# Upper channels stored with one DMA each, and the last six outputs shared among three engines and two queues

## The reference, cut to what matters

```python
x = x + conv(_ln_c(x), w_sym)
t = _to_tokens(x)
# _quantize_activations_groupwise, for a group ag of 3 images:
gamma = jnp.max(jnp.abs(ag))
xq = jnp.clip(ag * 128.0 / (gamma + EPS), -128.0 + EPS, 128.0 - EPS)
# _L0_ffn_ref
h = gelu(quantize(_ln_t(t) @ sign(W1).T + b1))
t = t + quantize(h @ sign(W2).T + b2)
```

## Time and profile before

| | |
|---|---|
| median of 3 runs | 613.7 us (611.32 to 615.29) |
| the profiled execution, its own time | 617.74 us |
| its span, first to last instruction | 615.9 us |
| mean granted clock of TensorE | 0.918 |
| TensorE busy | 496.8 us (81%) |
| VectorE busy | 467.1 us (76%) |
| ScalarE busy | 382.0 us (62%) |
| GpSimd busy | 219.7 us (36%) |
| moved by DMA | 81.29 MB, 132 GB/s over the span |

### The profile page before, as it was taken

How to read it: one execution, slowest core, us unless ns; L and a number is a source line. 1 busy time by engine, 2 the same in 40 slices (tenths; PEclk the granted TensorE clock), 3 DMA queues, 4 the chain that set the end, 5 groups by cost and what they waited for, 6 DMA issues and landing times.

```text
span 615.9 us, 9847 instructions
## 1 busy us (share of the span) xinstructions
PE 496.8 (81%) x3552; PEld 353.5 (57%) x3552; DVE 467.1 (76%) x1041; ACT 382.0 (62%) x598; POOL 219.7 (36%) x221
## 2 busy tenths in 40 slices
PE   2355527999969996758789989998999999987893
PEld 2255527999969995324335545555555555545562
DVE  7987861222228987996799898799989989699675
ACT  2688950000000353637799989998999898989550
POOL 4000000000400002212076747576666567558450
PEclk9666759999979997979999989999999999999798
DMA  8998325566965646940011000122222423263345
GB/s 223 290 316 248 104 61 150 149 175 169 204 161 150 178 124 250 386 157 1 27 51 53 27 27 0 52 82 74 78 74 77 133 78 101 80 230 104 125 135 178
DMA packets 55280, 81.29 MB, mean 132 GB/s; under 512 B 7361, under 2 KB 39105, under 8 KB 55232
## 3 DMA queue, kind: packets, MB, share of 16 engines
q1 hardware_dynamic: 39616, 68.28, 36.5%
q10 hardware_dynamic: 15136, 11.22, 6.5%
q0 software_dynamic: 480, 1.17, 0.9%
HBM read 53.12 MB, written 27.53 MB: 131 GB/s over the span
## 4 chain that ended last, share of the span: by engine, by line
PE 42%; DVE 22%; ACT 18%; DMA 10%; issue 5%; SPq 3%; ACTq 0%; DVEq 0%
PE bank L976 19%; DMA arena<-x 6%; PE bank L1058 5%; ACT arena L566 5%; DVE am L844 5%; ACT arena L560 4%; DMA arena<-kz_d 3%; PE bank L1026 3%; PE bank L1027 3%; PE bank L1028 3%; PE bank L1068 2%; DVE arena L816 2%; DVE arena L831 2%; ACT arena L482 2%; DVE arena L766 2%
## 5 line engine op out<-in xcount | busy, mean ns | idle before, releaser
L435 POOL TENSOR_TENSOR arena<-arena 128x512 f16<-128x512 f32 x159 | 186.9, 1212 | 120.6 <-DVE arena L831 99.3
L976 PE MATMUL bank<-arena 128*128 128x112 f32 (+1 forms) x1152 | 136.1, 283 | 20.8 <-ACT arena L482 12.6
L560 ACT ACTIVATE arena<-bank,b1s 128x512 f32<-128x512 f32 x180 | 125.1, 703 | 42.2 <-PE bank L1028 41.8
L976 PEld LDWEIGHTS bank<-arena 128*128 128x128 f32 x1152 | 135.0, 199 | 21.7 <-ACT arena L482 12.8
L1058 PE MATMUL bank<-arena 128*128 128x512 f16 x360 | 106.4, 390 | 5.4 <-ACT arena L584 3.6
L566 ACT ACTIVATE arena<-arena,gm 128x1024 f32<-128x1024 f32 x90 | 102.7, 1163 | 1.7 <-DVE gm L866 1.7
L844 DVE TENSOR_REDUCE am<-arena 128x1 f32<-128x3072 f32 x30 | 100.3, 3343 | 3.5 <-ACT arena L560 3.5
L750 DVE TENSOR_TENSOR arena<-bank,arena 128x512 f32<-128x512 f32 x48 | 33.2, 691 | 81.0 <-PE bank L976 80.9
L1026 PE MATMUL bank<-arena 128*128 128x512 f16 x180 | 71.0, 395 | 26.0 <-DVE arena L824 17.7
L497 ACT ACTIVATE arena<-arena,wmean 51x576 f16<-51x576 f32 (+1 forms) x10 | 8.6, 856 | 129.0 <-DVE wmean L724 116.2
L1027 PE MATMUL bank<-arena 128*128 128x512 f16 x180 | 70.6, 392 | 0.0
(11 more groups left out here) (118 smaller groups left out, 684.9 us busy)
## 6 DMA issues: line engine op xcount, KB each, us to landing
arena<-park_d SPq DMA_DIRECT2D x44, 384.0 KB, 3.6
arena<-kz_d SPq DMA_DIRECT2D x100, 112.0 KB, 2.9
arena<-kz_d ACTq DMA_DIRECT2D x92, 112.0 KB, 3.4
park_d<-arena SPq DMA_DIRECT2D x6, 1536.0 KB, 14.5
arena<-x SPq DMA_DIRECT2D x8, 1024.0 KB, 8.9
out<-arena SPq DMA_DIRECT2D x32, 256.0 KB, 2.0
kz_d<-arena SPq DMA_DIRECT2D x8, 672.0 KB, 11.0
arena<-x SPq DMA_DIRECT2D x16, 256.0 KB, 9.8
```

The source lines that it names most:

```text
L435: last = pool.tensor_tensor(out=low_half(u, m, m + 1), in0=yslot(u)[:, 2 * m:2 * m + 2, :], in1=hib(u, m, m + 1), op=ALU.subtract)
L560: act.activation(yslot(s)[:, 2 * m:2 * m + 2, :], m1p[c % 2][:, :].rearrange("p (h n) -> p h n", h=2), ACT.Identity, bias=b1s[:, m:m + 1], ...
L976: last = t.matmul(ps[:, :, lo:hi], WB[BUFS[g]][:, 1 - db, c, :], xn[:, :, lo + db:hi + db], start=(db == 0), stop=(db == -1))
```

## The change

Four things are changed. `store_upper` issues one DMA for both quarters, with the destination written as quarter, channel, pixel and the source as 128 partitions; it is used for all 30 units and for image 15, and the counts of the slots' semaphores change from 48 to 32. The two halves of image 15 have a semaphore each. Of the last six units, SyncE issues both stores of 24, 25 and 28, and ScalarE both of 27, 26 and 29. Units 25 and 26 are no longer finished by VectorE: ScalarE copies their turned inputs from PSUM to SBUF (keep_x, at steps 37 and 38, ahead of result(28) and result(29)), multiplies their outputs by the factor once it is known, and GpSimd adds the two. The turned inputs of units 28 and 29 use the banks of 25 and 26, and TensorE waits for the copies (xt) and no longer for fin.

```diff
-        turned = {... ((bank[0], bank[1]), (tA, tB), (m2a, m2b), (xA, xB), (bank[0], bank[1])))}
+        turned = {... ((bank[0], bank[1]), (tA, tB), (m2a, m2b), (bank[0], bank[1]), (tA, tB)))}
+        by_pool = early[0:2]
+        by_act = [early[2], early[1], early[4]]
+        XT = [view(XB + i * OW, OW) for i in range(2)]
+        def made(u):
+            return (fin_g, by_pool.index(u) + 1) if u in by_pool else (fin, u + 1 - sum(k < u for k in by_pool))
         def store_upper(q, u, slot, done):
-            for e in range(2):
-                at = u % 2 * HALF + e * QTR
-                q.dma_start(out[u // 2, P:C, at:at + QTR], Y2[e * C1:(e + 1) * C1, slot, HALF:OW]).then_inc(done, 16)
+            q.dma_start(out[u // 2, P:C, u % 2 * HALF:(u % 2 + 1) * HALF].rearrange("c (e n) -> e c n", e=2),
+                        Y2[:, slot, HALF:OW]).then_inc(done, 16)
 # sync: store(), and the loop
-                if u not in early:
-                    store_upper(sp, u, slot, done)
+                store_upper(sp, u, slot, done)
-                if 0 <= u < FT:
-                    sp.wait_ge(fin, u + 1)
+                if 0 <= u < FT and u not in by_act:
+                    sp.wait_ge(*made(u))
 # gpsimd, at its end
+            for i, u in enumerate(by_pool):
+                pool.wait_ge(xt, 2 * (i + 1))
+                pool.wait_ge(scaled, i + 1)
+                y = Y2[:, u % Y2R, :]
+                pool.tensor_tensor(out=y, in0=y, in1=XT[i], op=ALU.add).then_inc(fin_g, 1)
 # scalar
+            def keep_x(i):
+                act.wait_ge(mm1, MT * FT)
+                act.wait_ge(xpl, i + 1)
+                ta, tb = turn(by_pool[i])
+                act.activation(XT[i][:, 0:HALF], ta[:, :], ACT.Copy).then_inc(xt, 1)
+                act.activation(XT[i][:, HALF:OW], tb[:, 0:QTR], ACT.Copy).then_inc(xt, 1)
+                if FT - 2 <= w < FT:
+                    keep_x(w - FT + 2)
                 if s > FT and 0 <= w < FT:
                     result(w, 0)
-            for u in early:
-                act.wait_ge(fin, u + 1)
+            act.wait_ge(gsc2, FT // GT)
+            for u in by_pool:
+                y = Y2[:, u % Y2R, :]
+                act.activation(y, y, ACT.Copy, scale=gm[:, 9:10]).then_inc(scaled, 1)
+            for u in by_act:
+                b, half = u // 2, u % 2
+                act.wait_ge(*made(u))
+                act.dma_start(out[b, 0:P, half * HALF:(half + 1) * HALF], Y2[:, u % Y2R, 0:HALF]).then_inc(st_o[u % Y2R], 16)
                 store_upper(act, u, u % Y2R, st_o[u % Y2R])
 # vector
             def final(u):
+                if u in by_pool:
+                    return
 # tensor
             for i in (3, 4):
-                pe.wait_ge(fin, early[i] - 3)
+                pe.wait_ge(xt, 2 * (i - 2))
```

More of the change, by code:

```diff
@@ L215, in build @@
         gmx2 = sem("gmx2"); gtr = [sem(f"gtr{i}") for i in range(2)]; gone = [sem(f"gone{i}") for i in range(2)]; gall2 = sem("gall2"); gsc2_t = sem("gsc2_t"); gsc2 = sem("gsc2")
-        xps = sem("xps"); xpl = sem("xpl"); ld_g = [sem(f"ld_g{i}") for i in range(GT - 1)]; fin = sem("fin"); f15 = sem("f15")
-        st_o = [sem(f"st_o{i}") for i in range(Y2R)]; st_f15 = sem("st_f15")
+        xps = sem("xps"); xpl = sem("xpl"); ld_g = [sem(f"ld_g{i}") for i in range(GT - 1)]; fin = sem("fin"); fin_g = sem("fin_g"); xt = sem("xt"); scaled = sem("scaled"); f15 = sem("f15")
+        st_o = [sem(f"st_o{i}") for i in range(Y2R)]; st_f15 = [sem(f"st_f15{h}") for h in range(2)]
         block = ctx.enter_context(nc.Block())
@@ L250, in build @@
         XE = [*XL, *(view(at + i * RB * C, RB * C).rearrange("p (n c) -> p n c", n=RB) for i in range(2))]
-        turned = {v: pair for v, pair in zip(early, ((bank[0], bank[1]), (tA, tB), (m2a, m2b), (xA, xB), (bank[0], bank[1])))}
+        turned = {v: pair for v, pair in zip(early, ((bank[0], bank[1]), (tA, tB), (m2a, m2b), (bank[0], bank[1]), (tA, tB)))}
+        by_pool = early[0:2]
[3 more added lines that the diff above has]
+            return (fin_g, by_pool.index(u) + 1) if u in by_pool else (fin, u + 1 - sum(k < u for k in by_pool))
         def turn(u):
@@ L348, in store @@
                 sp.dma_start(out[b, 0:P, half * HALF:(half + 1) * HALF], Y2[:, slot, 0:HALF]).then_inc(done, 16)
-                if u not in early:
-                    store_upper(sp, u, slot, done)
+                store_upper(sp, u, slot, done)
             for h in range(2):
                 sp.wait_ge(f15, 2 * (h + 1))
-                store(FT + h, Y2R - 2 + h, st_f15)
+                store(FT + h, Y2R - 2 + h, st_f15[h])
             sp.wait_ge(st_pk[KEPT // 2], 16)
@@ L379, in _ @@
             for r in range(Y2R):
-                sp.wait_ge(st_o[r], 48 * len(range(r, FT, Y2R)))
-            sp.wait_ge(st_f15, 96)
+                sp.wait_ge(st_o[r], 32 * len(range(r, FT, Y2R)))
+            for done in st_f15:
+                sp.wait_ge(done, 32)
         @block.gpsimd
@@ L579, in result @@
                     if u >= Y2R:
-                        act.wait_ge(st_o[u % Y2R], 48 * (u // Y2R))
+                        act.wait_ge(st_o[u % Y2R], 32 * (u // Y2R))
                     elif u >= Y2R - 2:
-                        act.wait_ge(st_f15, 48 * (u - Y2R + 3))
+                        act.wait_ge(st_f15[u - Y2R + 2], 32)
                     act.wait_ge(mm2[0], u + 1)
```

## The result

The changed kernel is slower: 642.87 us (median of 6 runs) against 614.43 (6 runs), ratio 1.044 (95% interval 1.040 to 1.048), or +28.4 us. The forecast was 629.9, range 623 to 640: the sign is right and so is the cause, the merged store on two DMA engines, but the time lies above the range, since half of the loss arises where the prediction saw almost none.

The account below looks back on a forecast made before the run. The end was taken as bound by bytes through the DMA engines, then store issues. Two engines' 25.2 us from 605.9, 0.3 landing and 0.7 closing gave 632.1 against 615.9, +16.2; carried to the median 629.9 us, range 623 to 640.

Parts of the forecast that it names:

- Two engines: Every merged upper store, in body and end, runs on 2 of the 16 DMA engines; chance 0.70.
- the order of the two walks: Merged store's destination has 2 outermost, its source 128; all transfers seen spread by 16 have multiples of 16 on both sides.
- The end: Stores of the last six units: 25.2 us of work for two engines from 605.9, +16.2 us (+12.8 to +20.2).
- the row cost: Upper stores on two engines: 55 ns per 1 KB row, so 3.5 us a store.
- The body: Before the end, one unit's 5.3 us on the two engines fits between stores 4.7 to 6 us apart; 0 to 1.3 us.
- The sum: Whole kernel: span ends at 632.1 against 615.9, +16.2 us; carried to the median, 629.9 us.
- Rival B: Two engines, and late bring_back loads stall TensorE in the body: 3 to 8 us more, median 636 to 642; chance 0.10.
- Rival C: One engine carries each merged upper store, 5.9 us each, over +35 us; chance 0.03.
- Rival A: Merged stores spread over sixteen engines, the end bound by bytes: -1.6 us, median 611.9; chance 0.17.
- The small terms: In the last units: ScalarE's copies hidden (0), its scalings about 0.8 us each, GpSimd's additions 1.75 us, shorter store queues.
- The last issue: End of ScalarE's store queue: last issue at about 610.0 and not 613.1, with twelve issues and not eighteen.
- no stall: VectorE's last two outputs: inputs of units 28 and 29 ready at 605.2 and 606.3, wanted at 606.0 and 607.1.

Follow-up runs that it names:

- odd_rows: Changed kernel with separate upper-quarter stores, each quarter of the last six units stored in parts of 40 and 24 rows; 614.2 us in one execution.
- split: Changed kernel with both quarters of every upper store in a DMA of their own again, all else as changed; 613.52 us, ratio 0.999.

## Why the prediction was right or wrong

- **Two engines: right.** The small packets (2 each), the share of 0.12 to 0.14 at 46 to 49 GB/s and, for the rule, odd_rows show it. The argument from the order of the two walks, put at 0.70 + 0.10 against 0.17 for sixteen engines, decided the sign. The Trainium skill, same page, section "Rules for kernel authors", also advises for two transfers to disjoint halves of the partitions to use one of 128 partitions. Here the other side of the merged transfer is walked with e, of size 2, outermost, and the measurement (1.044) goes against following that advice in such a case.
- **The end: right in kind, 2.9 us too large.** The sum had 25.2 us of work for the two engines from 605.9, +16.2 in all (+12.8 to +20.2); measured +13.3. The term that was off is the row cost: 55 ns were taken, the middle of 46 and 65. At 46 to 49 GB/s over two engines a row of 1 KB takes 42 to 45 ns. The lower bound, 46 ns from the rate of the large rows, would have given 12.8. (The 86 ns for a row of 2 KB is in no row that the prediction shows; twice 46 gives the same 0.7 us for a lower store.)
- **The body: the step that failed.** "In the body ... That is 5.3 us late in the kernel ... It just fits" weighs the two engines' work against the time between stores, and allows 0 to 1.3 us for one load. The measured cost is 12.3 us between units 0 and 14; TensorE also waits 2.2 us for the input of unit 24, a cost that the middle stretch does not show apart from its own variation. Two things were wrong in it: it asked for throughput, where one load in a loop decides; and it looked at bring_back, late in the kernel, and not at bring_on, which VectorE waited for already. The row for it, 8.2 us of waits at L816, was in the list of waits and not used. A load behind a merged store lands 2.6 us later; VectorE waits for it at eight steps, each of which is 0.8 to 2.3 us longer than before, and that is the 12 us.
- **The sum.** Forecast +16.2, less the 2.9 at the end, plus the 12.3 in the body and 1.6 between units 14 and 24, is +27.2, and +28.4 were measured; the rest is within what single traces and medians vary by.
- **Rival B** named stalls in the body at 0.10, and its time (636 to 642) is near the measured one. But its mechanism was again lack of throughput for bring_back, "five to nine units" late in the kernel. The loss arose earlier and by another path, so B was not right either. The range ended at 640, inside B's own 642.
- **Rival C** has a slip that decides nothing: 35 us is the work that the upper stores' rows give one engine, and by the prediction's own sum (605.9 + 35.4 + 1.0 - 615.9) the end would grow by 26.4 us from them, not by over 35.
- **Rival A** (sixteen engines, 611.9) is the run split: -0.7 us by the ratio, against -1.6. The trace's own end became 1.1 us shorter.
- **The small terms: right but for two, neither of which costs anything here.** ScalarE's copies, the scalings at 0.88 against 0.8 and GpSimd's additions at 1.80 against 1.75 are as forecast. The last issue is not: it came 10.7 us behind the first output and not 6.1, with the two engines behind. The other one: TensorE idled from 609.7 to 611.9 for unit 24, and the granted clock, 1.00 until 612, was at its lower level of 1.2 GHz (0.50) from 613 to 619, while the inputs of 27 to 29 were turned back. Four transposes took 1.06 to 1.12 us there and not 0.60, and VectorE, for which "no stall" was forecast, waited 0.57 and 0.22 us for the last two; under the two engines' 22 us neither shows.

## What to carry to other kernels

Before two transfers are made one, write down the outermost size of both sides. In every count of this case the largest number up to 16 that divides both was the number of small packets that the transfer left, and with an outermost 2 two DMA engines carried it in place of sixteen. So count the small packets in the profile, and look at the share of the engines when nothing else moves. And when a transfer gets slower, don't ask only whether the queue keeps up; look for what is issued behind it on the same queue, and whether someone already waits for that. (Whether a load issued on another queue would be spared was not run.)

## What the runs showed of the hardware

- A transfer from SyncE's or ScalarE's queue with outermost size 128 or 64 leaves 16 small packets and one with 2 leaves 2; parts of 40 and of 24 rows together leave 22 (10 and 12 by the rule).
- A DMA engine that carries mostly 1 KB rows while fourteen others are idle moves 23 to 24.5 GB/s (46 to 49 GB/s over two, 628 to 636 in the changed kernel), one row in 42 to 45 ns; with all sixteen busy the same rows cost up to 65 ns (small packets counted in).
- A load over sixteen engines behind a store on two ends late on two of its engines only: fourteen of its small packets came by 407.2, the last two behind 408.0, and it counts as landed with the last.
- An edit of one index, a load issued a step earlier, took the body from 156.4 to 142.5 us with the slow stores still in place, the same 142.5 as without them.
